# Moving elementwise work to GpSimd, reordering VectorE and TensorE work, and four steps per loop body in a Mamba-2 mixer

## The reference, cut to what matters

```python
def layer(h, Wi, cw, cb, dtb, Alog, Dh, gw, Wo):          # h is rmsnorm(h) of the layer's input
    z, xBC, dt = split(h @ Wi)                            # 256, 512 and 8 columns
    conv = cb + sum(xp[:, k:k + L, :] * cw[:, k] for k in range(4))      # four taps
    xs, Bm, Cm = split(silu(conv))                        # 256, 128, 128 columns
    dt = softplus(dt + dtb); dA = exp(dt * -exp(Alog)); dtx = dt[..., None] * xs
    hs = hs * dA_t + dtx_t * B_t; y = sum_n(hs * C_t)     # scan over the tokens
    y = y + Dh * xs                                       # the skip sum
    y = rmsnorm(y * silu(z), gw)
    return y @ Wo                                         # added to h
```

## Time and profile before

| | |
|---|---|
| median of 3 runs | 1163.69 us (1159.37 to 1164.06) |
| the profiled execution | 1162.99 us, span 1161.0 us |
| PE, DVE, ACT, POOL busy | 86%, 84%, 76%, 58% of the span |
| granted TensorE clock, mean | 0.952 |

### The profile page before, as it was taken

One profiled execution on the slowest core, in us unless ns is written; L12 is line 12 of the kernel. 1 busy time (PEld: TensorE's weight loads), 2 busy tenths in 40 slices (PEclk: granted clock), 3 DMA queues, 4 the chain that ended last, 5 costly groups with the idle time before them and its releaser, 6 DMA issues.

```text
span 1161.0 us, 25184 instructions
## 1 busy us (share of the span) xinstructions
PE 993.7 (86%) x6136; PEld 559.7 (48%) x6136; DVE 977.1 (84%) x1801; ACT 884.2 (76%) x1724; POOL 676.3 (58%) x853
## 2 busy tenths in 40 slices
PE   5799999999899999999999999985788767999980
PEld 4244544445444444454445444542444445777760
DVE  6779999999999999999999998974778775888865
ACT  5688999999899999999999999984556534655640
POOL 0267577766776677656655765672244551666661
PEclk9789999999999999999999999998888888999995
DMA  5111242224222432210001000100000115676638
GB/s 141 34 34 33 89 156 86 88 87 153 91 86 87 142 102 86 78 32 22 22 23 31 22 22 23 27 7 1 19 28 28 37 33 180 223 232 226 223 116 217
DMA packets 85584, 97.84 MB, mean 84 GB/s; under 512 B 20698, under 2 KB 65888, under 8 KB 85536
## 3 DMA queue, kind: packets, MB, share of 16 engines
q1 hardware_dynamic: 80544, 88.83, 24.2%
q0 software_dynamic: 4992, 8.48, 2.2%
HBM read 59.67 MB, written 37.83 MB: 84 GB/s over the span
## 4 chain that ended last, share of the span: by engine, by line
PE 35%; DVE 26%; issue 18%; ACT 6%; POOL 3%; DVEq 2%; DMA 1%; ACTq 0%; SPq 0%; POOLq 0%
DVE cv L1354 9%; PE bank L494 4%; PE bank L562 4%; PE bank L681 2%; PE bank L667 2%; DVE M L1370 2%; PE bank L683 2%; PE bank L682 2%; DVE cv L1350 2%; PE bank L619 2%; PE bank L693 2%; PE bank L695 2%; PE bank L692 2%; PE bank L658 2%; PE bank L640 2%
## 5 line engine op out<-in xcount | busy, mean ns | idle before, releaser
L1354 DVE SCALAR_TENSOR_TENSOR cv<-bank,PAR,cv 128x511 f32<-128x511 f32 (+2 forms) x384 | 274.1, 742 | 15.7 <-ACT cv L963 2.8
L1370 DVE SCALAR_TENSOR_TENSOR M<-E,bank 128x512 f32<-128x512 f32 x256 | 168.3, 678 | 20.7 <-ACT E L951 11.4
L1679 POOL TENSOR_TENSOR yt<-yt,ti 128x384 f32<-128x384 f32 x64 | 64.0, 1000 | 203.6 <-DVE ti L1470 203.6
L494 PE MATMUL bank<-hn,WA 128*128 128x512 f32 x256 | 144.9, 649 | 41.0 <-DVE cv L1354 40.6
L951 ACT ACTIVATE E<-bank 128x512 f32<-128x512 f32 x256 | 149.0, 595 | 31.9 <-DVE M L1370 30.1
L1710 POOL DMA_INDIRECT RS<-y,XR x92 | 98.8, 1074 | 78.7 <-DVE y L1567 55.4
L1703 POOL DMA_INDIRECT XS<-stage,IDX x64 | 65.9, 1029 | 79.2 <-DVE run L1329 62.1
L1101 ACT ACTIVATE hr<-bank,W1B 128x512 f32<-128x512 f32 x92 | 63.4, 689 | 56.7 <-PE bank L683 49.8
L562 PE MATMUL bank<-M,dtx 128*32 128x128 f32 x2048 | 82.9, 279 | 15.6 <-DVE o_sb L1389 15.1
L494 PEld LDWEIGHTS bank<-hn,WA 128*128 128x128 f32 x256 | 40.6, 194 | 111.9 <-issue 74.0
L1497 DVE TENSOR_TENSOR hL<-hr,hH 128x512 fp32r<-128x512 f32 x124 | 87.1, 702 | 4.3
(11 more groups left out here) (245 smaller groups left out, 2633.8 us busy)
## 6 DMA issues: line engine op xcount, KB each, us to landing
XS<-PADT SPq DMA_DIRECT2D x32, 520.0 KB, 4.3
WA<-w_in SPq DMA_DIRECT2D x192, 64.0 KB, 1.8
W1B<-WD SPq DMA_DIRECT2D x23, 514.0 KB
W2B<-WD SPq DMA_DIRECT2D x23, 512.5 KB
WD<-WS SPq DMA_DIRECT2D x16, 512.0 KB, 2.7
XR<-XS SPq DMA_DIRECT2D x23, 260.0 KB
RW<-w_in SPq DMA_DIRECT2D x18, 256.0 KB, 4.4
WO_raw<-w_out SPq DMA_DIRECT2D x32, 128.0 KB, 3.6
```

Source lines behind the costliest of these rows:

```text
L494: mm(bank[t % 2][:, :], WA[t][:, :], hn[:, :], start=True, stop=True).then_inc(pj_mm, 1)
L1354: stt(out=cv[t][:, s:L], in0=src[:, 0:L - s], scalar=PAR[:, bass.ds(cw + 3 - s, 1)], in1=cv[t][:, s:L], op0=ALU.mult, op1=ALU.add).then_in ...
L1370: stt(out=M[i % 4][:, :].rearrange("p (n t) -> p n t", n=4), in0=E[i % 2][:, :].rearrange("p (n t) -> p n t", n=4), scalar=1.0, in1=bank[5 ...
```

## The change

- VectorE: the last tap of tile 0 comes directly behind its third; `causal_products` moves ahead of tile 1's third tap.
- VectorE: the two products `stmp` (line 1451) go to GpSimd; the skip sums (line 1465) stand between the parts of the chain of states, one ahead of each sum.
- TensorE: `project_out` comes ahead of `project(3)`.
- ScalarE: the squares of h, the copy of `WDT` and the scaling of `WO` go to GpSimd. The squares are made a step earlier than before.
- All engines: loops of 7 iterations with four bodies each, in place of 14 with two.

```diff
-        def pairs_of_steps(eng, body, first, last, **kw):
+        def fours_of_steps(eng, body, first, last, **kw):
-            with eng.Fori(first // 2, last // 2) as i:
-                for odd in (1, 0):
-                    k = eng.snap(2 * i + (2 - odd))
-                    body(k, odd, A=True, B=True, C=True, N=True, **kw)
+            with eng.Fori(first // 4, last // 4) as i:
+                for n in range(4):
+                    k = eng.snap(4 * i + (3 + n))
+                    body(k, (3 + n) % 2, A=True, B=True, C=True, N=True, **kw)
...
# SyncE
-                    wait(sp, wos_a, 2 * j)
+                    wait(sp, wos_p, 2 * j)
...
# TensorE
-                    wait(pe, wdt_a, k + 1)
-                    wait(pe, s_v, 5 * j - 2)
+                    wait(pe, wdt_done, k + 1)
+                    wait(pe, s_v, 3 * j - 1)
...
-                if A:
-                    project(3)
                 if C:
                     project_out()
+                if A:
+                    project(3)
...
-                    wait(pe, sqh_a, k + 2)
+                    wait(pe, sqh_done, k + 2)
...
-                    wait(pe, s_v, 5 * j + 5)
+                    wait(pe, s_v, 3 * j + 3)
...
# ScalarE
-            def norm_square(n):
-                wait(act, dt_mm, n)
-                f(WDT[:, :], PAR[:, bass.ds(n // NB * NPAR + C_WDT, 32)], ACT.Copy).then_inc(wdt_a, 1)
-                wait(act, hup, n + 1)
-                wait(act, ms_mm, n)
-                f(sqh[:, :], h[:, bass.ds(n % NB * L, L)], ACT.Square).then_inc(sqh_a, 1)
...
-                    wait(act, s_v, 5 * j - 1)
+                    wait(act, decay_p, 2 * j)
...
-                if N:
-                    norm_square(k + 1)
...
-                    wait(act, s_wo, 16 * (j + 1))
-                    wait(act, out_mm, j)
-                    gw = act.snap(j // NB * NPAR + C_GW)
-                    for t in range(2):
-                        f(WO[:, t * DM:(t + 1) * DM], WO_raw[:, t * DM:(t + 1) * DM], ACT.Copy,
-                          scale=PAR[:, bass.ds(gw + t, 1)]).then_inc(wos_a, 1)
...
# VectorE
                     tap(0, 2)
+                    tap(0, 3)
                     tap(1, 1)
-                    tap(0, 3)
+                if B:
+                    causal_products()
+                if A:
                     tap(1, 2)
                 if B:
-                    causal_products()
                     apply_decay(0)
...
+                    def with_skip(t):
+                        wait(dve, y_mm, 4 * j + 4)
+                        wait(dve, fin_p, 4 * j - 2 + 2 * t)
+                        stt(out=yt[t][:, :], in0=conv_rows(t, odd + 1), scalar=PAR[:, bass.ds(pj + C_D + t, 1)],
+                            in1=bank[6 + t][:, :], op0=ALU.mult, op1=ALU.add).then_inc(fin_v, 1)
                     cp(S[1][:, :], bank[4][:, 0:DI]).then_inc(s_v, 1)
-                    wait(dve, dec_a, j + 1)
                     for c in range(2, NC):
-                        wait(dve, s_v, 5 * j + 2 * c - 3)
-                        tt(stmp[:, :].rearrange("p (h d) -> p h d", h=NH), S[c - 1][:, :].rearrange("p (h d) -> p h d", h=NH),
-                           dec[:, (c - 1) * NH:c * NH].unsqueeze(2).to_broadcast([P, NH, HD]), ALU.mult).then_inc(s_v, 1)
-                        wait(dve, s_v, 5 * j + 2 * c - 2)
+                        with_skip(c - 2)
+                        wait(dve, decay_p, 2 * j + c - 1)
...
-                    for t in range(2):
-                        if t == 0:
-                            wait(dve, y_mm, 4 * j + 4)
-                        wait(dve, fin_p, 4 * j - 2 + 2 * t)
-                        stt(out=yt[t][:, :], in0=conv_rows(t, odd + 1), scalar=PAR[:, bass.ds(pj + C_D + t, 1)],
-                            in1=bank[6 + t][:, :], op0=ALU.mult, op1=ALU.add).then_inc(fin_v, 1)
...
# GpSimd
+            def square_h(n):
+                hb = h[:, bass.ds(n % NB * L, L)]
+                wait(pool, hup, n + 1)
+                wait(pool, ms_mm, n)
+                tt(sqh[:, :], hb, hb, ALU.mult).then_inc(sqh_done, 1)
+            def step_weights(n):
+                wait(pool, dt_mm, n)
+                tt(WDT[:, :], PAR[:, bass.ds(pool.snap(n // NB * NPAR + C_WDT), 32)], ones_row[:, 0:32], ALU.mult).then_inc(wdt_done, 1)
+            def output_weights(n):
+                gw = pool.snap(n // NB * NPAR + C_GW)
+                wait(pool, s_wo, 16 * (n + 1))
+                wait(pool, out_mm, n)
+                for t in range(2):
+                    tt(WO[:, t * DM:(t + 1) * DM], WO_raw[:, t * DM:(t + 1) * DM], PAR[:, bass.ds(gw + t, 1)].to_broadcast([P, DM]),
+                       ALU.mult).then_inc(wos_p, 1)
...
                 if A:
                     own_rows(0)
                     own_rows(1)
+                if N:
+                    step_weights(k + 1)
+                if B:
+                    output_weights(j)
+                if N and not B:
+                    square_h(k + 2)
                 if B:
+                    wait(pool, dec_a, j + 1)
+                    for c in range(2, NC):
+                        wait(pool, s_v, 3 * j + c - 1)
+                        tt(stmp[:, :].rearrange("p (h d) -> p h d", h=NH), S[c - 1][:, :].rearrange("p (h d) -> p h d", h=NH),
+                           dec[:, (c - 1) * NH:c * NH].unsqueeze(2).to_broadcast([P, NH, HD]), ALU.mult).then_inc(decay_p, 1)
+                    if N:
+                        square_h(k + 2)
                     for t in range(2):
                         wait(pool, fin_v, 4 * j + 3 + t)
```

More of the change, by code:

```diff
@@ L200, in build @@
         s_wo, p4_in = sem("wo_in"), sem("p4_in")
[L201 removed]
+        wdt_done, hup, sqh_done, ms_mm, rb_a, hn_v = sem("wdt_done"), sem("hup"), sem("sqh_done"), sem("ms_mm"), sem("rb_a"), sem("hn_v")
         dt_mm, pj_mm, silu_a, dtc_v, dta_a, tr_mm = sem("dt_mm"), sem("pj_mm"), sem("silu_a"), sem("dtc_v"), sem("dta_a"), sem("tr_mm")
         up_a, da_a, part_p, step_p = sem("up_a"), sem("da_a"), sem("part_p"), sem("step_p")
[L204 removed]
+        g_v, below_p, own_p, decay_p = sem("g_v"), sem("below_p"), sem("own_p"), sem("decay_p")
         g_mm, t_mm, t_ev, d_mm, e_a, m_v, y_mm = sem("g_mm"), sem("t_mm"), sem("t_ev"), sem("d_mm"), sem("e_a"), sem("m_v"), sem("y_mm")
         px_p, st_mm, s_v, e2_mm, e2_a, yi_mm = sem("px_p"), sem("st_mm"), sem("s_v"), sem("e2_mm"), sem("e2_a"), sem("yi_mm")
[L207 removed]
+        fin_v, fin_p, wos_p = sem("fin_v"), sem("fin_p"), sem("wos_p")
         sq_a, ss_mm, ry_a, out_mm, o_v = sem("sq_a"), sem("ss_mm"), sem("ry_a"), sem("out_mm"), sem("o_v")
@@ L239, in steps @@
             body(2, 0, A=True, B=True, C=True, N=True)
-            pairs_of_steps(eng, body, 3, STEPS - 1)
+            fours_of_steps(eng, body, 3, STEPS - 1)
             body(STEPS - 1, 1, A=True, B=True, C=True, N=False)
@@ L250, in steps_with_weights @@
             body(2, 0, A=True, B=True, C=True, N=True, W="shared")
-            pairs_of_steps(eng, body, 3, 3 + NE, W="up")
-            pairs_of_steps(eng, body, 3 + NE, 3 + 2 * NE, W="down")
-            pairs_of_steps(eng, body, 3 + 2 * NE, STEPS - 1)
+            fours_of_steps(eng, body, 3, 3 + NE, W="up")
+            fours_of_steps(eng, body, 3 + NE, 3 + 2 * NE, W="down")
+            fours_of_steps(eng, body, 3 + 2 * NE, STEPS - 1)
             body(STEPS - 1, 1, A=True, B=True, C=True, N=False)
@@ L436, in _ @@
             pe.wait_ge(const_v, 2)
-            pe.wait_ge(sqh_a, 1)
+            pe.wait_ge(sqh_done, 1)
             mm(bank[0][:, :], mean128[:, :], sqh[:, :], start=True, stop=True).then_inc(ms_mm, 1)
@@ L446, in square_mean_of_h @@
                 if n == 1:
-                    wait(pe, s_v, 5 * STEPS)
+                    wait(pe, s_v, 3 * STEPS)
                 else:
@@ L506, in project_out @@
                 def project_out():
-                    wait(pe, wos_a, 2 * (i2 + 1))
+                    wait(pe, wos_p, 2 * (i2 + 1))
                     if B:
@@ L569, in body @@
                     wait(pe, silu_a, 6 * j + 6)
-                    wait(pe, s_v, 5 * j)
+                    wait(pe, s_v, 3 * j)
                     for c in range(NC):
@@ L595, in body @@
                     square_mean_of_h(1)
+                if C:
+                    project_out()
                 if A:
                     project(3)
-                if C:
-                    project_out()
                 if C and not B:
@@ L866, in _ @@
             modulate_input(0, 0)
-            norm_square(0)
+            f(WDT[:, :], PAR[:, C_WDT:C_WDT + 32], ACT.Copy).then_inc(wdt_done, 1)
+            act.wait_ge(hup, 1)
+            f(sqh[:, :], h[:, 0:L], ACT.Square).then_inc(sqh_done, 1)
             for b in range(1, 4):
@@ L1028, in body @@
                     f(ecs[:, :], cum[:, :], ACT.Exp, scale=-1.0, bias=cum[:, CH - 1:CH]).then_inc(dta_a, 1)
-                if N:
-                    norm_square(k + 1)
-                elif A:
```

(3 more changed lines are left out.)

3 lines of the change are left out of this document (removed).

## The result

The changed kernel takes 1209.65 us (median of 6 runs, 1206.85 to 1212.73); the one before, beside it, 1161.53 us (6 runs). The ratio is 1.042 (95% interval 1.039 to 1.045): slower, as forecast, but by 48 us in place of 20, and nearly 11 us beyond the upper end of the range. The profiled execution took 1207.81 us, with a span of 1206.0.

What follows compares the result with a forecast made beforehand. It took a loop of dependences across TensorE, VectorE and ScalarE as the bound, not one engine's busy share. Terms 24.8 - 1.5 - 3.5 = +19.8 on 1162.99 us gave 1183 us for the median, range 1159 to 1199.

Steps and rivals of the forecast that it cites:

- Four bodies: Loop branches on all engines: 13 become 6, saving 7 x 0.5 us, -3.5 us.
- The clock is no term of the sum: In the mixer's loop the granted clock is 1.00, TensorE's upper level, so nothing was counted for it.
- `spend`: VectorE's small product, held by GpSimd's residual in bodies with expert weights: -1.5 us, from -3 to +12.
- the longer loop is fetched anew: Rival at the loop's branches: code doesn't stay on chip, 11 to 22 us more, 1199 us; chance 0.12.
- The recurrence: Chain of states S on VectorE and GpSimd: first tap 0.8 us later a step, 31 times, +24.8 us.
- the step back from GpSimd: Handover from GpSimd's product to VectorE's sum in the chain of S: 0.15 us, between 0.08 and 0.30.
- the lost cover: With skip sums gone from behind the states, nothing on VectorE covers TensorE's line 658, which takes 1.50 us.
- ScalarE's relief: Squares, `WDT` and `WO` leave ScalarE, some 1.3 us a step: gain 0, as the logarithm waits for TensorE's mean.
- Taps, output projection: Reordered taps and masks on VectorE, `project_out` ahead of `project(3)` on TensorE: 0; taps between -0.3 and +0.3 us.
- GpSimd's new work: Squares, two products, `WO` and `WDT` on GpSimd: 3.7 us a step, fits in its 6.45 us wait for `ti`; price 0.
- ScalarE sets the pace: Rival: ScalarE's lost 1.3 us comes off each step at the logarithm, -20 us, 1143 us; chance 0.17.
- absorbed: Rival: the skip sum's wait was idle time or the mean comes earlier; -5 to +3 us, 1163 us; chance 0.08.

Runs made afterwards that it cites:

- `before_fours`: The kernel before with only the loop changed, to four bodies in place of two on all engines: 1182.38 us, ratio 1.019.
- `after_pairs`: The changed kernel with its loops of two bodies again: 1184.96 us, ratio 1.023 against the kernel before.
- `fours_vector`: The kernel before with the loop of four bodies on VectorE alone, two on the other engines: 1184.62 us, ratio 1.022.
- written out: The loop's 28 steps stand one behind the other, with no branch: kernel before 1139.64 us (0.983), changed kernel 1161.86 us (1.002).
- `skip_between`: The changed kernel without loop branches, both `stmp` products back on VectorE, skip sums still between the parts of the chain: 1179.28 us, ratio 1.017.
- `rec_undone`: The changed kernel without loop branches, both `stmp` products back on VectorE and both skip sums behind the chain: 1144.53 us, ratio 0.985.
- `taps_only`: The kernel before without loop branches, plus only the change's order of taps, mask and output projection: 1144.42 us, ratio 0.986.
- `fours_scalar`: The kernel before with the loop of four bodies on ScalarE alone, two on the other engines: 1182.28 us, ratio 1.018.

## Why the prediction was off, step by step

- **Four bodies: this step failed.** It had seven branches less, at 0.5 us each, -3.5 us, and let the six that stay keep their price. The seven are worth that, but the other six cost 37 us in place of 3: VectorE stands for 3.3 to 5.8 us at each, ScalarE for up to 4.3, while code is fetched, and then TensorE runs at the lower clock. "The clock is no term of the sum" failed with it: it held for the kernel before, and the prediction didn't ask what a standing TensorE does to it. Isolated: +23 us (`before_fours` against before) and +22 to +25 (after against `after_pairs`, by the ratios and by the medians), where -3.5 for the branches and -1.5 for `spend` stood. That is the whole miss of some 27 us.
- **The rival "the longer loop is fetched anew"** had the mechanism, with a chance of 0.12, and came near in size: 1199 us, 16 us on top of the forecast, where some 27 were missing. It had one or two fetches a branch at 1.8 us, the time of a load of 64 KB. `fours_vector` shows 2.4 to 2.6 us from the fetch to the first instruction, and ahead of it 0.5 to 2.9 us; what came too low was the time per branch (28.0 us in six, 4.7 for each, in the changed kernel) and the lower clock, which the rival didn't have. The 4 fetches of the earlier trace rows only say that a body of two fits; I took from them that nothing spoke for or against, and gave 0.55 to the forecast as if the branch's price were independent of the length.
- **The recurrence: right.** +0.8 us a body; measured 23.60 - 22.90 = +0.70 in the profile (6.36 - 5.44 = +0.92 from `hn` to tap, -0.21 from tap to `o_sb`), +26 us in all with pairs, +22 written out, against 24.8. The wait for `within(3)` is 0.82 us where 0.6 was forecast, the step back from GpSimd at most 0.02 where 0.15 was taken, so the two errors partly cancel; TensorE waits for S, and `ti` for line 658. That the lost cover is what costs is shown by `skip_between`.
- **ScalarE's relief: right, 0.** `lnm` starts on TensorE's mean as before, and from `o_sb` to it there are 4.78 us before and after (565.97 - 561.19, and 559.34 - 554.56). `rec_undone`, which keeps the relief, is 0.43 us a body faster than `taps_only`, but all of it is the length of `cum`, by the rows and by the bodies of `skip_between`. No run moved `cum` by itself.
- **Taps, output projection: right, 0** (`taps_only`).
- **GpSimd's new work: right that it fits**; it waits 1.12 us for `ti` with all of it done.
- **`spend`: right in sign.** -1.5 us forecast; with expert weights a body of before was 0.25 us longer than one without (mean of 23.82 and 23.00 against that of 23.42 and 22.89), after 0.06, so some 3 us over 16 bodies, the favourable end of its range. By the changed order alone it would have been worse: in `after_pairs` it takes some 1155 ns in every second body, and a body takes 24.28 us with expert weights against 23.91 without. With fours it takes some 0.51 us in every one of these bodies, also behind a branch, where the forecast had it held: that part is luck. `hn` was held by 0.2 us at most in the changed kernel (928 ns), hidden as forecast.

The rivals "ScalarE sets the pace" and "absorbed" are ruled out by `after_pairs`: without the loop the change is 2.3% slower, not 2% faster or the same.

## What to carry to other kernels

When a loop's body is made longer, ask first whether each engine's share of it still stays on the chip. The profile shows it by the count of instruction fetches inside the loop, against the number of branches, by "issue" ahead of the first instruction behind the branch, and by a granted clock that falls behind it; one engine whose body doesn't fit costs what all of them would. Between a loop that fits and straight code without a branch there may be no good middle: 1159 us with pairs, 1182 with fours, 1140 with none, for the same work. And work that looks as if it merely fills time behind a chain may be what hides the next engine's part of it: find out what it covers before it is moved forward.

## What the runs showed of the hardware

- With a body of four, a taken branch made VectorE alone stand 2.9 and 3.2 us with idle DMA engines and 4.7 to 5.3 with full ones (`fours_vector`), and ScalarE alone 3.2 to 4.6 us at the first four branches (`fours_scalar`); as many fetches in straight code showed no wait at all.
- Behind each of these branches TensorE stood for some microseconds (6.0 at 387 us in `fours_vector`), and its granted clock was then 0.50 for 3.4 to 10.2 us. With pairs or written out it stayed at 1.00 through the loop.
- VectorE and GpSimd hold each other up in more forms than the `spend` of the earlier trace rows. The instruction that starts second gets longer: `cum` 0.44 to 0.88 us, `stmp` 0.42 to 1.14, and `hn` 0.75 to 1.38 us in `rec_undone`, where it starts 0.21 us behind `sqh`:

```profile
578.20 1.38 DVE L1463 SCALAR_TENSOR_TENSOR hn<-h,PAR,rB 128x512 f32<-128x512 f32 x1
```
```profile
577.99 1.05 POOL L1610 TENSOR_TENSOR sqh<-h 128x512 f32<-128x512 f32 x1
```

All three have both inputs in SBUF. The Trainium skill ("SBUF — State Buffer", SBUF: two separate sides) says that for such instructions, and the rows agree that the later one is held. They fall a little short of the skill's "fully blocks": `sqh` ends at 579.04, `hn` takes 0.75 us alone, and ends at 579.58 and not at 579.79. The Trainium skill also says that VectorE's instructions with one SBUF input contend only in their 2-port modes; that the strided `spend` (290 ns alone, 1175 beside `WS`) was held too does not settle it, since its mode isn't in the trace.
- Such a hold is set by a few hundredths of a microsecond: `cum` starts 0.01 us behind GpSimd's product and takes 0.44 us longer. It repeats in 26 of the 28 bodies of `taps_only`'s loop, and can flip from one to the next, as in `skip_between`; so a median can hide a gain or a loss of 10 us that no edit aimed at.
